# Attention with key chunks of 128, 128 and 68 and query chunks of 68, 128 and 128, and another order of steps

## The reference

```python
h = _L0_tok_ref(x, L0_tok_W, L0_tok_b)               # 196 patches of 768 values -> 256
h = jnp.concatenate([h, txt], axis=1)                # 324 tokens
h = h + _L0_attn_ref(_layernorm(h, axis=-1), Wq, bq, Wk, bk, Wv, bv, Wo, bo)
h = h + _L0_ffn_ref(_layernorm(h, axis=-1), w_gate, w_up, w_down)
# _L0_attn_ref:
att = jnp.einsum('bhqd,bhkd->bhqk', q, k) * scale
att = jnp.where(mask, att, jnp.float32(-jnp.inf))    # causal
att = jax.nn.softmax(att, axis=-1)
y = jnp.einsum('bhqk,bhkd->bhqd', att, v)
```

## Time and profile before

| | us |
|---|---|
| median of three runs | 2053.52 |
| lowest, highest | 2045.04, 2055.91 |
| profiled execution, device time | 2044.34 |
| its span, first to last instruction | 2042.5 |
| `phase_a` | the first 1400, about |
| `phase_b` and its start | the rest |

### The profile page before, as it was taken

One profiled execution on the slowest core, in us unless ns is written; L12 is line 12 of the kernel. 1 busy time (PEld: TensorE's weight loads), 2 busy tenths in 40 slices (PEclk: granted clock), 3 DMA queues, 4 the chain that ended last, 5 costly groups with the idle time before them and its releaser, 6 DMA issues. The chain is left out here.

```text
span 2042.5 us, 37905 instructions
## 1 busy us (share of the span) xinstructions
PE 1781.4 (87%) x14552; PEld 1471.4 (72%) x14552; DVE 1627.8 (80%) x3188; ACT 961.4 (47%) x1646; POOL 872.1 (43%) x971
## 2 busy tenths in 40 slices
PE   3698888988888888888888888887499999999998
PEld 3477666776666766666776676664389999999997
DVE  5667788777887778877788787875399999999998
ACT  1255555555555555455554565554233333333333
POOL 5445555555555555555555555552012121121211
PEclk8899999899998999999999899997699999999999
DMA  3544554445544455444554445540211111111111
GB/s 104 92 70 71 91 87 94 81 71 90 88 90 85 71 88 87 86 93 71 87 91 86 89 71 88 78 75 21 66 52 58 58 57 60 58 60 58 60 58 47
DMA packets 140650, 152.45 MB, mean 75 GB/s; under 512 B 20279, under 2 KB 135607, under 8 KB 140471
## 3 DMA queue, kind: packets, MB, share of 16 engines
q1 hardware_dynamic: 133558, 149.02, 37.4%
q10 hardware_dynamic: 6912, 1.00, 0.3%
HBM read 51.25 MB, written 34.01 MB: 42 GB/s over the span
## 5 line engine op out<-in xcount | busy, mean ns | idle before, releaser
L605 DVE TENSOR_REDUCE maxima<-maxp 108x2 f32<-108x648 f32 (+2 forms) x448 | 415.6, 928 | 235.9 <-PE maxp L946 235.8
L828 ACT ACTIVATE probs<-expp 108x648 f32<-108x648 f32 (+2 forms) x512 | 363.7, 710 | 271.0 <-PE expp L971 257.3
L507 POOL TENSOR_SCALAR_AFFINE_SELECT probs<-probs 108x216 f32<-108x216 f32 (+1 forms) x512 | 286.4, 563 | 381.1 <-ACT probs L828 380.2
L1189 POOL TENSOR_TENSOR hq<-q_b,scale_b 128x704 f32<-128x704 f32 x81 | 112.6, 1390 | 471.0 <-DVE q_b L1246 471.0
L943 PE MATMUL maxp<-kst,qst 96*108 96x108 bf16 (+2 forms) x1536 | 279.6, 275 | 18.3 <-DMA kst<-parts 10.8
L971 PE MATMUL expp<-qst,kst 99*108 99x324 bf16 (+2 forms) x1536 | 251.8, 274 | 44.2 <-DMA qst<-negparts 33.8
L943 PEld LDWEIGHTS maxp<-kst,qst 96*108 96x108 bf16 x1536 | 179.1, 137 | 71.4 <-issue 23.5
L971 PEld LDWEIGHTS expp<-qst,kst 99*108 99x108 bf16 x1536 | 151.1, 134 | 106.4 <-DMA qst<-negparts 43.4
L992 PE MATMUL attp<-probs,vblk 108*32 108x324 f32 (+2 forms) x3072 | 223.2, 388 | 2.5 <-POOL probs L507 1.5
L946 PE MATMUL maxp<-mask_qk,identb 108*108 108x108 bf16 (+2 forms) x896 | 222.8, 255 | 0.0
L59 PE MATMUL gu<-wgu_hi,xqT_hi 128*128 128x512 f32 (+1 forms) x486 | 191.4, 394 | 2.0 <-DVE xqT_lo L1201 2.0
(11 more groups left out here) (183 smaller groups left out, 4499.6 us busy)
## 6 DMA issues: line engine op xcount, KB each, us to landing
qst<-parts SPq DMA_DIRECT2D x192, 162.0 KB, 5.1
kst<-parts SPq DMA_DIRECT2D x192, 162.0 KB, 5.9
patches<-in_xT SPq DMA_DIRECT2D x32, 588.0 KB, 4.6
h_dram<-h_rows SPq DMA_DIRECT2D x32, 324.0 KB
xq_dram<-x_n SPq DMA_DIRECT2D x32, 324.0 KB
xq<-xq_dram SPq DMA_DIRECT2D x81, 128.0 KB, 2.0
res<-h_dram SPq DMA_DIRECT2D x81, 128.0 KB, 2.1
out_rows<-ot SPq DMA_DIRECT2D x81, 128.0 KB, 1.7
```

The costliest lines, as they stand in the source:

```text
L507: pool.affine_select(out=at, in_=at, compare_op=ALU.is_ge, fill=0.0, base=0, pattern=[[0, nh], [1, CH]], channel_multiplier=-1).then_inc(p ...
L605: dve.tensor_reduce(rowmax[half][:, h:h + nh, c].rearrange("p (a h) -> p a h", a=2), src, AX.X, ALU.max).then_inc(maxp_free, 1)
L828: act.activation(dst, expp[0:CH, 0:banks, 0:per * w], ACT.Exp, scale=SCALE).then_inc(expp_free, 1)
L1189: pool.tensor_tensor(blocks(hq[t % 2][:, 0:FF]), blocks(q[:]), spread(scale[:], P, NB_H), ALU.mult).then_inc(hq_done, 1)
```

## The change

Keys go in chunks of 128, 128 and 68. Queries are padded by 60 columns in front (`QPAD`), so that their chunks hold 68, 128 and 128 real queries. A chunk of queries then meets 68, 196 or 324 keys, a chunk of keys 324, 196 or 68 queries. `qst` grows from 324 to 384 columns a head, of which the first 60 are cleared once by POOL. The rows of tokens (`h0`, `xn`, `att`, the projection) stay in chunks of 108. The number of instructions of each kind on PE, DVE and ACT doesn't change.

```diff
+QPAD = NC * P - T
+KEYS = [(i, min(i + P, T)) for i in range(0, T, P)]
 def width(c):
-    return CH * (c + 1)
+    return P * (c + 1) - QPAD
+
+def queries(kc):
+    return T - KEYS[kc][0]
...
-        vblk = [sb(f"vblk{i}", [CH, NC, H, VW]) for i in range(2)]
-        qst = [sb(f"qst{i}", [P, H, T], BF16) for i in range(2)]
+        vblk = [sb(f"vblk{i}", [P, NC, H, VW]) for i in range(2)]
+        qst = [sb(f"qst{i}", [P, H, NC * P], BF16) for i in range(2)]
...
-                                sp.dma_start(stack[p][row:row + HD, :, :],
+                                sp.dma_start(stack[p][row:row + HD, :, QPAD if stack is qst else 0:],
                                              parts[:, part, t:t + 2, :]).then_inc(stack_in[p], 16)
...
+            pool.wait_ge(weights_split, 4)
+            for s in qst:
+                pool.memset(s[:, :, 0:QPAD], 0.0).then_inc(padded, 1)
...
-                            pe.matmul(maxp[0:CH, a, x * w:(x + 1) * w], qst[other][0:ROWS, h, c * CH:(c + 1) * CH],
+                            pe.matmul(maxp[:, a, x * w:(x + 1) * w], qst[other][0:ROWS, h, c * P:(c + 1) * P],
                                       kst[other][0:ROWS, h, 0:w], start=x == 0, stop=False, skip_group_check=True)
...
-                            ins = pe.matmul(expp[0:CH, a, x * w:(x + 1) * w],
-                                      kst[s][0:ROWS + NPART, h, kc * CH:(kc + 1) * CH],
-                                      qst[s][0:ROWS + NPART, h, kc * CH:T], start=x == 0,
+                            ins = pe.matmul(expp[0:hi - lo, a, x * w:(x + 1) * w],
+                                      kst[s][0:ROWS + NPART, h, lo:hi],
+                                      qst[s][0:ROWS + NPART, h, QPAD + lo:], start=x == 0,
```

The table `STEPS` is written anew, with the same steps. Its first and last lines:

```diff
-    ("h0b",), MAX_A[0], ("x2 stats",), ("xnT", 0), ("attend", 1, 0), ("exp", 2, 0), MAX_A[1], ("xnT", 1), ("tok", 1),
+    ("x2 stats",), ("tok", 1), MAX_A[0], ("xnT", 0), ("xnT", 1), ("attend", 1, 0), ("x2 root",), ("exp", 2, 0),
...
-    ("xn",), ("exp", 1, 3), ("w", 8), ("proj", 1),
+    ("proj", 1), ("exp", 1, 3), ("w", 8),
```

More of the change, by code:

```diff
@@ new lines @@
+    MAX_B[2], ("tok", 1), ("exp", 0, 1), ("attend", 3, 1), ("attend", 3, 2), ("w", 4), ("w", 5), ("x2 out",),
+    MAX_B[3], ("exp", 0, 2), ("turn", 0), ("tok", 1), ("patches",), ("exp", 0, 3), ("h0",), ("patches lo",), ("v", 0),
+    ("last", 0), ("root",), ("exp", 1, 0), ("turn", 1), ("attend", 0, 0), MAX_B[4], ("exp", 1, 1), ("turn", 2),
+    ("v", 1), ("last", 1), MAX_B[5], ("attend", 0, 1), ("turnback", 0), ("xn shift",), ("turnback", 1), ("exp", 1, 2),
+    MAX_B[6], ("attend", 0, 2), ("w", 6), ("v", 2), ("neg", 1), ("xn",), ("proj", 0), ("w", 7), ("neg out", 1),
@@ L375, in prob_lo @@
         def prob_lo(kc, head):
-            return 4 * sum(T - CH * i for i in range(kc)) + head * (T - CH * kc)
+            return 4 * sum(queries(i) for i in range(kc)) + head * queries(kc)
         def lin_of(k, step):
@@ L1035, in body @@
                 if k.attends:
+                    if n == 1:
+                        pe.wait_ge(padded, len(qst))
                     pe.wait_ge(stack_in[other], STACK_DMAS * (k.half + p))
```

72 lines of the change are left out of this document (35 added, 37 removed).

## The result

The changed kernel takes 2019.94 us (median; 2015.1 to 2020.85) where the kernel before takes 2052.78 on the same chip (2045.04 to 2055.91): a ratio of 0.9849, 95% interval 0.9824 to 0.9873. It is faster by 33 us, inside the range, and the forecast was 88. The profiled execution spans 2017.7 us.

A forecast was written before the change was run, and what follows sets the result against it. PE was taken as nearest to full, DVE close behind. Per image, -6.8 us of waits, clock and work plus 1.4, 1.8, 0.4 and 0.6 gave -2.6, 42.3 to 39.7; over 31 images 81 us, so 1965 us, range 1860 to 2035.

The forecast's parts named there:

- ("exp", 0, 0): PE's wait for the first half's small transfers: path 6.4 to 7.1 us, cover 5.0, so +1.4 us an image.
- The turn of the second half: PE's turn of the second half's maxima, waiting for DVE: the sum had no term for it.
- both terms of the clock: PE's granted clock: 1.6 us an image regained with the old idle time, 0.6 lost to new waits (bounds 0 and 3).
- The wait for `xn`: PE before the turn of `xn`, waiting for ACT: the new order removes 2.9 us an image.
- the one before the projection: PE before the projection's second half, waiting for DVE to empty a bank: 1.2 us an image goes.
- The work: Fewer columns on PE in scores and products with v: 1.1 us an image saved, bounds 0.7 and 1.3.
- The big stack transfers in the same place: Large copies in the same engines as the small transfers before ("exp", 0, 0): up to 3 us more wait.
- the last rival: The order doesn't pay: DVE's hidden stalls return beside `patches_lo`, 2.7 us an image, 2033 to 2054; no change given 0.07.
- The start of the iteration: PE waits at the iteration's head for the stack transfers, behind POOL's chain: +1.8 us an image, bounds 0 and 5.
- ("exp", 2, 0): PE's wait for the second half's small transfers, issued after `xn`: +0.4 us an image, bounds 0 and 1.5.
- the waits only change place: Rival: new waits take the clock down in most images, +2.0 us instead of +0.6; 2007 to 2035 us.
- clock down, gain small: Outcome class of 2000 to 2043 us, given a chance of 0.15.

The follow-up runs named there:

- chunks_only: The changed kernel's new chunks with the table of steps of the kernel before; 2017.88 us, ratio 0.9836 to the kernel before.
- order_only: The old chunks of 108 with the changed kernel's new table of steps; 2032.36 us, ratio 0.9899 to the kernel before.
- rest_late: The changed kernel with POOL's ("rest", 1) moved behind the split of the maxima and ("exp", 3, 3); 1969.99 us, ratio 0.9587 to the kernel before.
- gate: The changed kernel with SP's stack copies held back until the first half's three small transfers have landed; 1955.24 us, ratio 0.9525 to the kernel before.
- late_nogate: rest_late with ("xn shift") moved behind POOL's second `last`, no wait added on SP; 1948.69 us, ratio 0.9505 to the kernel before.
- rest_shift: rest_late with ("xn shift") put one step earlier on DVE, ahead of ("turnback", 0); 1984.07 us, ratio 0.9662 to the kernel before.
- shift_late: The changed kernel with the changes of rest_late and gate, and ("xn shift") moved behind POOL's second `last`; 2005.58 us, ratio 0.9776 to the kernel before.

## Why the prediction was right in sign and wrong in size

It is told an image at a time. The forecast was -2.6 from a period of 42.3; measured is -0.9 over all images (41.7 to 40.8) and -1.2 in the 28 whole ones (42.56 to 41.37), which lie nearer to that 42.3. Three steps failed. The path to ("exp", 0, 0) was lengthened by what stands on ACT alone, and POOL beside DVE made it longer (8.8 us, not 7.1). The turn of the second half was put at nothing and waits 1.05 us more. And both terms of the clock were too small, which nearly cancelled.

- **The wait for `xn` (-2.9) and the one before the projection (-1.2): right.** Neither is left, though the second was the chunks' doing, as chunks_only shows, and not the order's; a wait of 10.7 us in sum (0.3 an image) for a bank of v is new at ("turn", 2).
- **The work (-1.1, bounds 0.7 and 1.3): right for the chunks.** PE's work goes from 34.45 to 33.10 us in chunks_only, -1.35, the upper bound. The new order costs 0.5 of it (34.45 to 34.99 in order_only), which the sum did not have; with both it is -0.8. DVE's maxima came as computed (0.72 and 0.97 forecast), and the weight loads of 128 columns are shorter than those of 108, 102 ns against 137:

```profile
L619 DVE TENSOR_REDUCE maxima<-maxp 128x4 f32<-128x784 f32 x128 | 125.0, 976 | 152.8 <-PE maxp L962 152.0
L619 DVE TENSOR_REDUCE maxima<-maxp 128x8 f32<-128x544 f32 x64 | 44.9, 702 | 10.8 <-PE maxp L962 10.7
```
```profile
L959 PEld LDWEIGHTS maxp<-kst,qst 96*128 96x128 bf16 x1536 | 124.7, 102 | 122.5 <-DVE maxima L619 59.3 <-issue 20.9
```
```profile
L943 PEld LDWEIGHTS maxp<-kst,qst 96*108 96x108 bf16 x1536 | 179.1, 137 | 71.4 <-issue 23.5 <-DVE maxima L605 14.8 <-DMA kst<-parts 11.6
```
Four matmuls of 68 columns take 0.14 us (909.08 to 909.22), 34 ns each, so the floor of 47 ns did not hold. By the rule of the Trainium skill quoted in the prediction (TensorE: Matmul & The Clock Gate, Weight-path perf modes) the upper bound was due, and the trace agrees.

- **("exp", 0, 0) (+1.4): right as a wait, wrong as a path.** The wait grew by (79.4 - 33.8) / 31 = 1.5. But the path is 8.8 us, not 7.1; 1.0 of the difference, (38.9 - 7.3) / 31, is idle time at the maxima group in the middle of it, which the sum does not have. The step that failed is "I add 0.6 to 0.9 to the path": it looked at what the new order puts on ACT and left out what it puts beside DVE's split on POOL. rest_late shows that this is the cause: the path reads 7.25 us there, and 50 us come back.

```profile
919.59 0.33 PE L971 MATMUL attp<-ident,maxima 128*128 128x128 f32 x1
...
926.84 0.45 PE L987 MATMUL expp<-qst,kst 99*128 99x324 bf16 x2 [1.91 <-DMA qst<-negparts]
```
- **The big stack transfers in the same place ("up to 3 more", of which the +1.4 takes little): in the bounds, priced too low.** What the earlier issue of the copies costs, and with it the clock, is gate's 65 us, or 2.1 an image, the largest single piece. It was there in the text as a bound; that the change moves ("exp", 3, 3), which lets the copies go, ahead of the third small transfer instead of behind it, was read but given no term.
- **The turn of the second half (0): missed, +1.05** ((48.2 - 15.6) / 31). The text put such a stall at ("w", 6), where the second `last` may run; the mechanism was right, the operation was the shift, some steps ahead of it, and the sum had nothing for either. late_nogate shows it for the shift (48.7 to 7.3 us in sum). It is also the warning of the last rival ("DVE's hidden stalls come back"), at half its price, on top of a smaller gain.
- **The start of the iteration (+1.8) and ("exp", 2, 0) (+0.4): did not come.** The chain on POOL was well forecast: from the last matmul of the embedding (923.02) to the end of the second `last` (931.96) are 8.9 us, forecast 0.4 + 0.9 + 2.7 + 1.4 + 0.9 + 1.0 + 1.4 = 8.7. But PE comes at 935.70, 12.7 us after that matmul and not 10.1: it waits 1.43 and 0.39 us on the way, of which 0.5 was forecast, and some 1.3 us of work had been counted short. The stall that was missed paid for the wait that was forecast. When the stall was taken away (late_nogate) the forecast wait stood there, 33.3 us in sum, 1.1 an image. The two ends, of the embedding and of the iteration, in the changed kernel:

```profile
923.02 0.28 PE L61 MATMUL tokp<-wtok_hi,patches_lo 128*88 128x256 f32 x1
...
935.70 0.35 PE L59 MATMUL tokp<-wtok_hi,patches_hi 128*108 128x256 f32 x1
```
- **The clock (-1.6 + 0.6 = -1.0): -0.8 in sum, but by luck.** Both terms were too small. Before, the clock cost 2.66 us an image and not 1.6. The text took 2.7 us of the low stretch for idle time, but most of the low stretch lies behind the wait: in the earlier trace rows it reads 0.81 in two microseconds in which PE mostly waits, and 0.50 later, with PE busy all the time. Of 6.1 us an image at the half level PE idles in 0.8. After, it costs 1.86 and not 0.6: 3.9 us at the half level, of which PE idles in 0.2. The text said that a wait between the 1.0 that did not take the clock down and the 2.7 that did would cost 0.6; with one of 2.34 it falls in nearly every image (26 times in 28 images). With gate the clock is 0.99.

In sum, in the 28 images: idle time +0.4, forecast -4.1 + 3.6 = -0.5; work -0.8, forecast -1.1; clock -0.8, forecast -1.0. Of the 1.4 us that the image missed 0.9 are idle time. The waits that the sum did not have (turn 1.1, maxima group 1.0, bank of v 0.4) come to 2.5 us, and the two that it had and that did not come would have been 2.2. The likeliest case was therefore named wrongly: it was the rival "the waits only change place" (2007 to 2035; "clock down, gain small" was given 0.15), by two stalls that it did not name. Its 2.0 us for the clock are near the 1.86 measured.

What POOL beside DVE does here was there to be read: w_y of 3.03 us in the earlier trace rows was told as the cause of two waits, and the rule was then applied to one line of the new order. The Trainium skill has it (SBUF — State Buffer, Who interferes with whom): a DVE instruction with two inputs in SBUF contends with a POOL instruction that reads SBUF, through a shared pair of ports that is an exclusive lock, and the order of issue decides which of the two is blocked. By that rule the split's subtraction and the shift, both with two such inputs, stall beside ("rest", 1) and `last`, and the traces agree (1.43 and 1.33 us).

That the first half's small transfers and the large copies share something is told by the runs (1.95 against 5.8 us). The Trainium skill says as much in a sentence (DMA: Bandwidth & Descriptors, Issuing engines are not separate DMA queues): transfers run on the same 16 engines and interleave, whichever engine issued them.

**What stays open.** That rest_late and gate don't add (50 and 65 us apart, 67 together) is told by the clock, which costs 0.8 us an image more with both than with gate alone. Why it falls behind one wait and not behind another of much the same length is open, and so is why it falls more often in rest_shift than in rest_late. Nor was it tried what the 7 us cost that ("exp", 0, 0) waits once in the first images (the largest value in the list of waits), or an issue of the last pair's copies ahead of other work.

## What to carry to other kernels

When an order of steps is changed, list for each engine what runs beside each small operation of the others, not only what stands ahead of it in its own queue: a 24x128 subtraction and a shift of three values beside POOL cost 50 and 21 us here, by the runs that moved one step alone. A small transfer on the critical path belonged ahead of the large ones here, and on top of the other repairs better by issue order (1908) than by a wait for its landing (2006). And a wait that is removed is worth nothing until it is known what is late next: rest_late gained 50 us alone and 2 on top of gate (1953 against 1955), and the shift moved late cost 53 on top of both (2006), until the start of the copies was moved as well (1908).

## What the runs showed of the hardware

- In rest_shift a DVE operation of three values a partition, begun beside POOL operations that follow one another without a gap, lasted until the last of them ended, not the first: 2.10 us through two masks and a `last`. Without POOL beside it (shift_late) it took 0.17.
- A transfer of 6 KB landed in 1.95 us without the large SBUF copies around it (gate). Its reader started 4.2 us after its issue where they were issued beside it, and 5.8 us where they were issued 1.9 us ahead.
- Six copies of 162 KB within SBUF an image took 1.9 us more of the 16 engines' time in pieces of 648 B than of 1296 B (share of the queue 47.0% and 51.4%), and the kernel the same time (1.0005).
- The length of one idle time did not tell by itself whether the granted clock fell. It read 0.50 after idle times of 2.34 (after) and 3.17 us (shift_late), and after 1.91 in rest_late, the first two rows below; it stayed at 1.00 through the 2.00 of rest_shift, the last two.

```profile
926.00:928.00 2.00, 1.16 (x11) 1.03 (x11) 0.11 (x1) 0.68 (x2) 0.00 (x0) 1.00 1.04 101
...
930.00:932.00 2.00, 2.00 (x13) 1.88 (x11) 0.89 (x2) 0.84 (x2) 1.24 (x2) 0.50 1.21 115
```
```profile
946.00:948.00 2.00, 0.29 (x9) 0.12 (x8) 2.00 (x2) 1.02 (x3) 2.00 (x4) 1.00 0.28 72
948.00:950.00 2.00, 1.41 (x9) 1.04 (x10) 2.00 (x6) 1.44 (x3) 0.39 (x1) 1.00 0.44 108
```
